# Graph attention on one core: queries in two PSUM banks and made two groups ahead, one-hots three ahead, exponentials and row numbers in SBUF, VectorE's additions last

## What is computed

```python
loops = jnp.arange(n); src = concat([src, loops]); dst = concat([dst, loops])
for l in range(L):                       # L = 2
    xn = layernorm(x); xp = xn + (xn @ Wpos + bpos + deg * Wdeg + bdeg)
    q, k, v = (xp @ Wq + bq, xp @ Wk + bk, xp @ Wv + bv)      # n x 8 x 16 each
    att = clip(einsum('ehd,ehd->eh', q[dst], k[src]) / scale, -50, 50)
    ex = exp(att - segment_max(att, dst)[dst])
    alpha = ex / segment_sum(ex, dst)[dst]
    x = x + segment_sum(v[src] * alpha, dst) @ Wo + bo
    x = x + gelu(layernorm(x) @ W1 + b1) @ W2 + b2
```

## Time and profile before

| | before |
|---|---|
| median of 3 runs | 2185.11 us |
| lowest, highest | 2184.74, 2186.89 us |
| span of the profiled execution | 2183.8 us |
| mean granted TensorE clock | 0.810 of full speed |
| VectorE busy | 1710.2 us (78%) |
| GpSimd busy | 1570.6 us (72%) |
| TensorE busy, matmuls | 1419.8 us (65%) |
| ScalarE busy | 940.2 us (43%) |

### The profile page before, as it was taken

How to read it: one execution, slowest core, us unless ns; L and a number is a source line. 1 busy time by engine, 2 the same in 40 slices (tenths; PEclk the granted TensorE clock), 3 DMA queues, 4 the chain that set the end, 5 groups by cost and what they waited for, 6 DMA issues and landing times.

```text
span 2183.8 us, 32409 instructions
## 1 busy us (share of the span) xinstructions
PE 1419.8 (65%) x8227; PEld 1237.3 (57%) x8227; DVE 1710.2 (78%) x5103; ACT 940.2 (43%) x2179; POOL 1570.6 (72%) x1669
## 2 busy tenths in 40 slices
PE   4866576666667676766666657566666757666666
PEld 4555565656555565655556556556555656555555
DVE  8759888888877878787877777777777778777775
ACT  8334353534535353534454335343343435343344
POOL 6277777777777777777727777777777777777773
PEclk9979888877878788887988787787787778787787
DMA  2365445444444444444424444444444444444441
GB/s 87 119 178 182 148 133 154 147 136 134 142 134 125 142 134 142 124 142 134 132 69 143 135 125 136 137 123 139 133 139 124 139 134 129 134 134 138 125 138 56
DMA packets 123505, 289.29 MB, mean 132 GB/s; under 512 B 31525, under 2 KB 57057, under 8 KB 123329
## 3 DMA queue, kind: packets, MB, share of 16 engines
q0 software_dynamic: 77824, 212.31, 33.8%
q1 hardware_dynamic: 45504, 74.92, 10.3%
HBM read 275.44 MB, written 8.38 MB: 130 GB/s over the span
## 4 chain that ended last, share of the span: by engine, by line
POOL 47%; issue 20%; DVE 11%; PE 11%; DMA 6%; ACT 3%; DVEq 1%; SPq 0%; ACTq 0%
POOL kvr L801 47%; DMA kvr<-kv_table,srcidx 5%; PE bank L1079 4%; PE bank L1092 3%; DVE agg L1706 3%; DVE kvr L1322 2%; DVE prod L1675 1%; DVE msg L1697 1%; ACT apart L1279 1%; ACT onehotT L1283 1%; DVE onehot L1667 1%; PE bank L1036 1%; PE bank L1015 1%; PE bank L816 1%; PE bank L894 1%
## 5 line engine op out<-in xcount | busy, mean ns | idle before, releaser
L801 POOL DMA_INDIRECT kvr<-kv_table,srcidx x1612 | 1530.7, 950 | 547.4 <-issue 480.0
L1079 PE MATMUL bank<-q,onehotT 128*128 x3320 | 606.8, 340 | 712.1 <-DVE prod L1675 475.2
L1079 PEld LDWEIGHTS bank<-q,onehotT 128*128 128x128 f32 x3320 | 515.6, 237 | 825.5 <-issue 824.8
L1092 PE MATMUL bank<-msg,onehot 128*128 128x136 f32 x3320 | 612.3, 344 | 1.9 <-DVE msg L1697 1.9
L1289 ACT ACTIVATE bank<-attc 128x32 f32<-128x32 f32 x404 | 81.2, 201 | 1145.7 <-DVE attc L1691 1145.0
L1092 PEld LDWEIGHTS bank<-msg,onehot 128*128 128x128 f32 x3320 | 571.8, 252 | 3.6 <-DVE msg L1697 3.3
L1675 DVE TENSOR_TENSOR prod<-kvr,bank 128x512 f32<-128x512 f32 x404 | 276.0, 683 | 302.6 <-DMA kvr<-kv_table,srcidx 264.0
L1706 DVE TENSOR_TENSOR agg<-agg,bank 128x136 f32 x1624 | 469.1, 289 | 44.9 <-PE bank L1092 40.1
L1279 ACT ACTIVATE apart<-relT,minus_p 128x512 bf16<-128x512 bf16 x416 | 293.8, 706 | 4.4 <-DMA relT<-rel_table 4.0
L1667 DVE TENSOR_TENSOR onehot<-bank,rel 128x512 f32<-128x512 f32 x416 | 282.5, 682 | 0.2
L1697 DVE TENSOR_TENSOR msg<-kvr,bank 128x512 f32<-128x512 f32 x404 | 273.9, 678 | 5.0 <-ACT bank L1289 4.9
(11 more groups left out here) (217 smaller groups left out, 844.5 us busy)
## 6 DMA issues: line engine op xcount, KB each, us to landing
relT<-rel_table SPq DMA_DIRECT2D x104, 512.0 KB, 4.1
kvr<-kv_table,srcidx POOLq DMA_INDIRECT x1612
loop_kv<-kv_table SPq DMA_DIRECT2D x25, 128.0 KB, 3.9
kv_table<-qkv SPq DMA_DIRECT2D x25, 128.0 KB, 3.2
kv_table<-onehot SPq DMA_DIRECT2D x8, 256.0 KB, 2.2
w<-weights SPq DMA_DIRECT2D x2, 840.0 KB, 7.4
loops<-x_in SPq DMA_DIRECT2D x5, 320.0 KB, 5.6
q<-qkv SPq DMA_DIRECT2D x25, 64.0 KB
```

What stands on the lines that cost most here:

```text
L801: pool.indirect_dma_start(kvr[:, n % RING, j, :], None, kv_table[l], bass.IndirectOffsetOnAxis(ap=srcidx[:, step:step + 1], axis=0)).then_ ...
L1079: mm = pe.matmul(bank[2][:, j * D:(j + 1) * D], onehotT[:, m % OHT, j, :], q[:, bass.ds(ranks[j + h], 1), :].rearrange("p a c -> p (a c)") ...
L1092: mm = pe.matmul(sum_ps(n, k), onehot[:, m % OH, j, :], msg[:, n % 2, j, :], start=(m, j) == of[0], stop=(m, j) == of[-1])
```

## The change

The queries of even groups go to bank 2, those of odd groups to bank 0, and TensorE makes them two groups ahead instead of one, waiting for the product of group n - 2. ScalarE makes the one-hots for them three groups ahead instead of two, and SyncE loads their rows one group earlier. `ex` moves from PSUM to SBUF, two buffers deep. `edge_onehot` compares with `iota_free` in SBUF, so the copy `iota_ps` in PSUM, its semaphore and its wait go. VectorE's iteration becomes: product of n, messages of n - 1, attention of n, one-hots of n + 2, clip, addition 0, guard, additions 1 to 3 (and 4).

```diff
-DVE_NEXT, ACT_NEXT = 6, (12, 16)
+DVE_NEXT, ACT_NEXT = 6, (12, 16, 17)
...
+        ex = sb("ex", [P, 2, G * H])
...
-        ex = bank[0][:, G * H:2 * G * H]
-        iota_ps = bank[0][:, P:2 * P]
+        q_ps = (bank[2], bank[0])
...
-                        if s < GROUPS and group_of((body - 1) * BODY - 1) - 1 == l * GROUPS + s:
+                        if s < GROUPS and max(group_of((body - 1) * BODY - 1) - 2, 0) == l * GROUPS + s:
                             rel_rows(body)
...
-                if n:
-                    pe.wait_ge(s_prod, n)
+                if n >= 2:
+                    pe.wait_ge(s_prod, n - 1)
                 for j in range(gathers(n)):
                     for h, m in enumerate(hots(n)):
-                        mm = pe.matmul(bank[2][:, j * D:(j + 1) * D], onehotT[:, m % OHT, j, :],
+                        mm = pe.matmul(q_ps[n % 2][:, j * D:(j + 1) * D], onehotT[:, m % OHT, j, :],
...
                 edge_q(l * GROUPS)
+                edge_q(l * GROUPS + 1)
                 for s in range(SLOTS):
                     n = l * GROUPS + s
-                    if s + 1 < GROUPS:
-                        edge_q(n + 1)
+                    if s + 2 < GROUPS:
+                        edge_q(n + 2)
...
-                act.activation(ex[:, 0:t * H], attc[:, n % 2, 0:t * H], ACT.Exp).then_inc(s_ex, 1)
+                act.activation(ex[:, n % 2, 0:t * H], attc[:, n % 2, 0:t * H], ACT.Exp).then_inc(s_ex, 1)
...
+            edge_spread(2)
             for l in range(L):
...
-                        if s + 2 < GROUPS:
-                            edge_spread(n + 2)
+                        if s + 3 < GROUPS:
+                            edge_spread(n + 3)
...
-                    dve.tensor_tensor(onehot[:, m % OH, :, :], iota_ps.unsqueeze(1).broadcast_to([P, G, P]),
+                    dve.tensor_tensor(onehot[:, m % OH, :, :], iota_free[:].unsqueeze(1).broadcast_to([P, G, P]),
...
                 edge_prod(n)
-                add(0)
                 if g >= 1:
                     edge_msg(n - 1)
-                add(1)
                 edge_att(n)
-                add(2)
+                if g + 2 < GROUPS:
+                    edge_onehot(n + 2)
                 edge_clip(n)
-                add(3)
+                add(0)
+                edge_guard(n)
+                for j in range(1, G):
+                    add(j)
                 if g >= 2 and is_seam(n - 2):
                     add(G)
-                if g + 2 < GROUPS:
-                    edge_onehot(n + 2)
-                edge_guard(n)
-
-            dve.tensor_copy(iota_ps, iota_free[:]).then_inc(s_iota_ps, 1)
```

More of the change, by code:

```diff
@@ L448, in build @@
         s_deg = sem("s_deg")
-        s_iota_ps = sem("s_iota_ps")
         s_wq = sem("s_wq")
@@ L1674, in edge_prod @@
                 t = gathers(n)
-                dve.tensor_tensor(prod[:, 0:t, :], kvr[:, n % RING, 0:t, 0:D], bank[2][:, 0:t * D].rearrange("p (j c) -> p j c", c=D), ALU.mult).then_inc(s_prod, 1)
+                dve.tensor_tensor(prod[:, 0:t, :], kvr[:, n % RING, 0:t, 0:D], q_ps[n % 2][:, 0:t * D].rearrange("p (j c) -> p j c", c=D), ALU.mult).then_inc(s_prod, 1)
             def edge_att(n):
@@ L1697, in edge_msg @@
                 dve.tensor_tensor(by_head(msg[:, n % 2, 0:t, 0:D]), by_head(kvr[:, n % RING, 0:t, D:KV]),
-                                  ex[:, 0:t * H].rearrange("p (j h) -> p j h", h=H).unsqueeze(3).broadcast_to([P, t, H, HD]), ALU.mult).then_inc(s_msg, 1)
+                                  ex[:, n % 2, 0:t * H].rearrange("p (j h) -> p j h", h=H).unsqueeze(3).broadcast_to([P, t, H, HD]), ALU.mult).then_inc(s_msg, 1)
             def edge_add(n, j, ranks):
@@ L1755, in _ @@
                     dve.wait_ge(s_first_table, 16 * len(KV_PAIRS))
-                    dve.wait_ge(s_iota_ps, 1)
                     for k in range(2):
```

## The result

The changed kernel takes 2261.15 us (median of four runs, 2257.36 to 2262.76) against 2185.9 before: a ratio of 1.0342, 95% interval 1.0327 to 1.0356. The forecast was 2252, with a range from 2215 to 2285. Sign, total and the mechanism of the dearest term were right; that term came out at 46 us instead of 63, and two fifths of the loss (31 of 77 us) came from where the prediction had booked 6 us or nothing. That the total is so near is in part luck.

A forecast was written before the change was run, and what follows sets the result against it. GpSimd's back-to-back gathers were taken as the bound, 1612 x 1.25 = 2021 us of 2183.8. Held gathers 63, layer-end lag 6, less 0.5 and 1.2, gave +67: span 2251, median 2252, range 2215 to 2285.

The forecast's parts named there:

- the dearest term: GpSimd's gathers held by messages and one-hots once both operands lie in SBUF: 63 us, bounds 20 to 89.
- The held gathers: Gathers starting inside a 128x512 VectorE instruction with two SBUF inputs wait till 0.56 us after its start: 0.155 x 404 = 63 us.
- A phase without rule: Groups starting with VectorE behind have no fixed phase against the gathers; held gathers cost them together 0.15 us each.
- The sparing of the one-hot: In the gated phase the gather after a held one starts at 2.41, just past the one-hot's hold at 2.36: nothing lost.
- The additions: VectorE's additions last, stepping by 0.44: +0.60 us an iteration, mostly hidden by idle time; 3 us per layer end, 6 in all.
- rival C: VectorE becomes the bound if the additions cost 0.85 us an iteration: 26 us more, 2278; chance 0.10.
- The other 3 us: VectorE's added lag at the end of layer two, 3 us of the 6 booked for both layer ends.
- Edits at nothing: Earlier queries, one-hots and row loads, the exponential's SBUF write and the dropped copy cost nothing; queries ready win 0.5 us.
- 63 + 6 - 0.5 - 1.2: Held gathers, layer-end lag, less a shorter ring gap at start-up and the guard coming earlier at both layer ends: +67 us.
- A (no lock): The two SBUF-operand instructions hold no gather and only the additions count: 2193; chance 0.08.
- B (faster): VectorE's lag at the layer ends vanishes and gathers keep 1.25 us: about -9 us, 2176; chance 0.05.
- D: GpSimd also holds VectorE for whole gathers, 0.36 us for each of two instructions: 184 us, 2369; chance 0.02.

The follow-up runs named there:

- the order alone: The kernel before with only VectorE's new order, operands in PSUM and queries one ahead: 2209.36 us, ratio 1.0115.
- the row load back: The changed kernel with SyncE's row load of layer two's third body back in layer two's first slot: 2247.65 us, ratio 1.0302.
- the register reads later: The changed kernel with VectorE's register reads for its additions behind the product instead of ahead of it: 2261.09 us, ratio 1.0360.

## Why the prediction was right, and where it was not

**The held gathers: mechanism right, size right where it was worked out.** A message holds a gather until 0.56 us after its start; it was read off two widths that the kernel before happened to have the earlier trace rows, and the table above has it to 0.01. In the waiting iterations, all of them in layer two, a group lost 0.16 us, as forecast; over all of layer two it was 0.14. One timeline piece of a waiting iteration shows the whole step: the gather starts 0.39 into the message and takes 0.16 more, and the next one starts 0.05 past the one-hot's hold.

```profile
1305.21 0.69 DVE L1660 TENSOR_TENSOR prod<-kvr,bank 128x512 f32<-128x512 f32 x1 [0.93 <-DMA kvr<-kv_table,srcidx]
1305.81 0.68 DVE L1682 TENSOR_TENSOR msg<-kvr,ex 128x512 f32<-128x512 f32 x1
1306.20 1.11 POOL L784 DMA_INDIRECT kvr<-kv_table,srcidx  x1 [0.30 <-issue]
1307.01 0.68 DVE L1652 TENSOR_TENSOR onehot<-iota_free,rel 128x512 f32<-128x512 f32 x1
1307.62 0.95 POOL L784 DMA_INDIRECT kvr<-kv_table,srcidx  x1 [0.30 <-issue]
```

The sparing of the one-hot, most in doubt, held: messages held 227 gathers (42.8 us), one-hots 7 (1.6). The term came out at 46 instead of 63, and 14 of these 17 us are missing in layer one, where VectorE was behind throughout: at its own period of 4.4 us a group lost only 0.09. "A phase without rule" was the step that failed: a VectorE that is behind has a rule of its own. Of the rows behind this term one was read too sharply. In the kernel before the 20 long gathers exceed 0.947 by 3.3 us together, not 3.9; four of them start inside other instructions, three in the 128x128 normalisation (L1528), which has one wide SBUF input, and the first in one that reads PSUM (L1742). The forecast does not hang on it.

**The additions: mechanism right, size short.** The steps of 0.44 came; the register reads ahead of prod, which waiting additions leave uncovered, did not stand in the sum. An iteration took 4.38 to 4.43 us instead of 4.14, +0.84 instead of +0.60 (by its own numbers, 4.14 - 3.57, the forecast had 0.57). The idle time of an iteration in layer one, 0.47 to 0.59 us, with the 0.09 by which a group grew does not cover that: the lag at its end is 20 us (prod of the last group at 1155.28, its last gather at 1132.58) and not 4.7 + 3. That is rival C's mechanism, in one layer, together with the forecast's. The other 3 us, booked for the end of layer two, did not come: prod of its last group is 1.9 us late in both kernels. With the order alone the lag cost 22 us of gap; the changed kernel with the row load back still has 14.5 over 34.7.

**"Edits at nothing" failed in two places.** Of SyncE's row loads the text said that they move ahead of table and output stores, "with the same lead over ScalarE", and priced that at nothing. The queue was named, the wait in front of the load was not followed to its release: 9 to 14 us. And TensorE's order "starts at the same instants" only where the queries do not wait; at the start they wait 12 us with sums behind them, with 4.9 us more of ring wait, where 0.5 were booked as a gain.

**The sum.** Forecast 63 + 6 - 0.5 - 1.2 = 67; measured 46 + 26 + 5 = 77, the gap being about 15 of lag and 12 of the blocked queue. The total is nearer than its terms, by two errors that offset each other: 17 us too much in the gathers, 21 too little in the gap and 5 in the ring. In part they hang together, since the lag that the additions caused also took the gathers off the message; the run with the register reads later shows this exchange, 16 us one way and 15 the other. The 12 us of the blocked queue have nothing to do with it, and that they filled the rest was luck.

**The rivals.** A (no lock) and B (faster) fell with the 46 us; the order alone, which is A made into a kernel, gave 2209.36 instead of A's 2193, for the register reads again. D, in which GpSimd holds VectorE for whole gathers, fell: one-hots that start inside a gather take 681 ns in the mean of 379, messages 685 in that of 329, as against 682 and 679 for such ones in the kernel before. With it falls, for this kernel, the half of the lock as the Trainium skill states it (SBUF — State Buffer, section "SBUF: two separate sides") that whichever starts first keeps the pair for its whole instruction; the VectorE side of it is what the runs show, for the first 0.56 us of a 128x512 instruction that lasts 0.68. Whether it is the gather's reading of its row numbers that waits was not tried. VectorE's work was not cheaper for SBUF operands either, 684 ns as against 682 and 678. By the Trainium skill, VectorE: DVE Perf Modes, section on the TRN2 errata, with its smaller fixed cost for an SBUF source, it would have been; the trace disagrees.

What the changed kernel would be with its operands in PSUM and queries two ahead was not tried: bank 0 now holds queries, and in the other banks TensorE would write beside them.

## What to carry to other kernels

Where gathers from GpSimd's queue set the pace, look at where each wide VectorE instruction with two SBUF inputs stands against their starts; in this kernel one PSUM operand left every gather at its length, and with both operands in SBUF the order alone moved the loss between 46 and 102 us. Before moving a transfer ahead in a queue, follow the wait in front of it to the instruction that releases it, and see what stands behind. An engine's slack is used once: additions that wait for each other, register reads that nothing covers and grown periods all drew on the same 0.6 us, and freeing some of it gave the time to the next collision.

## What the runs showed of the hardware beyond that

A gather that starts together with a VectorE instruction of two SBUF inputs (up to 0.03 us into it, with two exceptions in all runs) is not held; one that starts from 0.04 to 0.55 us into it is held to 0.56 after that instruction's start, for 128x512. The other way round VectorE loses next to nothing: the messages' mean went from 678 to 684 ns. Three additions that wait for each other step by 0.44 us, spread ones take 0.20 of the iteration. Register reads that follow waiting additions cost VectorE 0.24 to 0.28 us (4.38 to 4.43 against 4.15), those behind spread ones nothing (3.55 in both kernels).
